# Graph layer with a mixture of experts on one core: the edge-row gathers run two groups ahead of the segment sums instead of four

## The reference

```
msg = feat[src]
agg = segment_sum(msg, dst, n)              # edges sorted by dst
deg = segment_sum(ones, dst, n)
x = x + feat @ W_self + (agg / max(deg, 1)) @ W_neigh + b        # feat = layernorm(x)
xn = layernorm(layernorm(x)) * gamma + beta
w = softmax of the two largest of (xn @ Wr + br)
x = x + sum over e of w[e] * (gelu(xn @ W1[e] + b1[e]) @ W2[e] + b2[e])
```

## Time and profile before

| | us |
|---|---|
| median of three runs | 1588.26 |
| lowest and highest | 1587.45, 1598.54 |
| span of the profiled execution | 1546.9 |
| mean granted TensorE clock | 0.908 |
| busy: TensorE, VectorE, ScalarE, GpSimd | 1199.9, 867.0, 426.8, 944.1 |

### The profile page before, as it was taken

How to read it: one execution, slowest core, us unless ns; L and a number is a source line. 1 busy time by engine, 2 the same in 40 slices (tenths; PEclk the granted TensorE clock), 3 DMA queues, 4 the chain that set the end, 5 groups by cost and what they waited for, 6 DMA issues and landing times.

```text
span 1546.9 us, 22459 instructions
## 1 busy us (share of the span) xinstructions
PE 1199.9 (78%) x6492; PEld 1041.8 (67%) x6493; DVE 867.0 (56%) x2814; ACT 426.8 (28%) x803; POOL 944.1 (61%) x1023
## 2 busy tenths in 40 slices
PE   0377988888977798989889888677858775879857
PEld 0266777867866676877778777566747764778747
DVE  6745556665564655656565565554636553545426
ACT  5412222222322332332332323213313210211111
POOL 6756656666566666566655657665665566666642
PEclk9788999999997899999999999788978897999979
DMA  9798777755454565555554555464565556656545
GB/s 335 232 297 247 244 230 239 238 166 173 152 166 124 164 190 160 181 172 171 188 182 157 181 157 164 135 191 133 165 204 157 167 158 199 201 165 222 167 139 175
DMA packets 175355, 289.69 MB, mean 187 GB/s; under 512 B 25600, under 2 KB 105344, under 8 KB 175104
## 3 DMA queue, kind: packets, MB, share of 16 engines
q1 hardware_dynamic: 124288, 156.38, 30.6%
q0 software_dynamic: 45504, 124.36, 27.3%
q10 hardware_dynamic: 5440, 7.47, 1.4%
HBM read 231.43 MB, written 56.68 MB: 186 GB/s over the span
## 4 chain that ended last, share of the span: by engine, by line
PE 33%; DVE 28%; another core or an unknown queue 21%; issue 12%; DVEq 2%; POOL 2%; DMA 1%; SPq 0%; ACT 0%; POOLq 0%; ACTq 0%
PE bank L1040 9%; PE bank L964 8%; PE bank L1066 6%; DVE agg L1311 5%; PE bank L1074 4%; DVE heap L1468 4%; DVE onehot L1257 3%; PE bank L952 2%; PE bank L993 1%; PE bank L995 1%; DMA heap<-in_x 1%; DVE nstats L1339 1%; DVE xf L1334 1%; DVE agg L1337 1%
## 5 line engine op out<-in xcount | busy, mean ns | idle before, releaser
L689 POOL DMA_INDIRECT ring<-feature_table,src_sb x760 | 742.3, 977 | 468.3 <-issue 194.6
L964 PE MATMUL bank<-ring,onehot 128*128 128x257 f32 x1552 | 404.0, 403 | 73.5 <-DMA rows<-in_x,src_sb 40.9
L964 PEld LDWEIGHTS bank<-ring,onehot 128*128 128x128 f32 x1552 | 312.1, 203 | 131.7 <-issue 83.4
L1468 DVE TENSOR_TENSOR heap<-bank,b_sb 128x512 f32<-128x512 f32 x145 | 100.1, 690 | 342.1 <-remote 249.7
L1066 PE MATMUL bank<-heap 128*128 x712 | 193.5, 418 | 60.4 <-issue 18.1
L1040 PE MATMUL bank<-row_t,heap 128*128 128x128 f32 x1424 | 195.9, 294 | 38.8 <-DVE heap L1468 19.3
L1040 PEld LDWEIGHTS bank<-row_t,heap 128*128 128x128 f32 x1424 | 186.6, 208 | 46.2 <-issue 45.0
L866 ACT ACTIVATE heap<-heap 128x512 f32<-128x512 f32 x145 | 91.6, 632 | 453.7 <-DVE heap L1468 312.7
L1066 PEld LDWEIGHTS bank<-heap 128*128 128x128 f32 x712 | 142.4, 208 | 86.0 <-issue 66.3
L1040 PE MATMUL bank<-dst_i,heap 128*128 128x128 f32 x896 | 115.8, 284 | 32.8 <-DVE heap L1468 25.9
L1257 DVE TENSOR_TENSOR onehot<-iota,target 128x512 f32<-128x512 f32 x196 | 134.3, 685 | 6.9 <-DVE xf L1328 3.5
(11 more groups left out here) (190 smaller groups left out, 1258.1 us busy)
## 6 DMA issues: line engine op xcount, KB each, us to landing
heap<-in_w SPq DMA_DIRECT2D x145, 512.0 KB
expert_out<-empty_row SPq DMA_DIRECT2D x68, 256.0 KB
ring<-feature_table,src_sb POOLq DMA_INDIRECT x760
row<-expert_rows SPq DMA_DIRECT2D x89, 128.5 KB
xf<-in_x SPq DMA_DIRECT2D x49, 128.0 KB
ff<-feature_table SPq DMA_DIRECT2D x49, 128.0 KB
expert_out<-inside SPq DMA_DIRECT2D x45, 128.0 KB
expert_out<-y_out SPq DMA_DIRECT2D x44, 128.0 KB
```

What stands on the lines that cost most here:

```text
L689: pool.indirect_dma_start(group_row(t, i)[:, 0:D], None, x if t < RAW else table, bass.IndirectOffsetOnAxis(src_sb[:, k:k + 1], 0)).then_i ...
L964: last = pe.matmul(bank[t % 2][:, 0:D + 1], onehot[:, q, i, :], group_row(t, i), start=(i == 0), stop=(i == GT - 1))
L1468: dve.tensor_tensor(hid[S.slot(u, 2)], hidden_b[:, :].rearrange("p (k t) -> p k t", k=HK), b1_sb[:, bass.ds(e, 1), :].rearrange("p o k -> ...
```

## The change

From group 10 on, the gather of group t waited until group t - 4 was summed, which is the group whose slot of the ring it takes. Now it waits until group t - 2 is summed. The ring keeps its four slots, and nothing else is changed; groups 6 to 9 wait as before.

```diff
 GT = 4
 GS = 4
+ROWS_AHEAD = 2
 LC = 7
...
             def gather(t):
                 g, q = NG - 1 - t, t % GS
                 if t >= RAW:
-                    pool.wait_ge(summed, (t - GS if t - GS >= RAW else t - RAW) + 1)
+                    pool.wait_ge(summed, (t - ROWS_AHEAD if t - GS >= RAW else t - RAW) + 1)
                 if t >= GS:
                     pool.wait_ge(gathered[q], 16 * GT * (t // GS))
```

## The result

The time falls from 1589.47 us to 1576.36 us (medians of four runs each); the ratio is 0.9891, 95% interval 0.9848 to 0.9933. The forecast was 1613 us, slower. The profiled execution after has a span of 1576.2 us and so stands at its own median. That of before, with 1546.9 us, stood 41 us under its median, so the two profiles can't be subtracted from one another. (The execution profiled after took 1578.0 us for its span of 1576.2, so only 1.8 us lie around a span.

The account below looks back on a forecast made before the run. TensorE and VectorE were taken to set each group's step, gathers running beside it. Stalls of 36.8 us less 12 given back made 24.8, added to the 1588.3 us median: 1613 us, range 1592 to 1648.

Parts of the forecast that it names:

- The edit really takes away room: Gathers from group 10 on: they start 11.6 us later on average over groups 17 to 195, losing about two thirds of their room.
- Start: Groups 10 to 12: gather 10 must wait for sum 8, 4.9 us later, all of it on the path.
- Bunches: Sums close together on TensorE: nine groups from 11 on lack the needed 7.0 us, together 13 us.
- the list: New gather starts carried through group by group: 28.6 us; 36.8 with later semaphore releases; 88.8 with two clocks mixed, too high.
- Given back: Behind late sums TensorE often waits anyhow, so a third of 36.8 us comes back: -12 us.
- two groups are enough: Rival, chance 0.30: nearly every stall is given back; +4 to +15 us, about 1597 us.
- Other work behind the gathers on GpSimd: Takes and row loads move later with the gathers: 3 us once for a take, not added; row loads 0.
- not slower: Rival, chance 0.05: in 85 to 150 us later gathers leave the DMA engines to weight loads; 1580 us.
- It does nothing: Rival, chance 0.02: GpSimd never was four groups ahead, so the edit changes nothing; 1588 us.
- delays compound: Rival, chance 0.13: stalls make GpSimd's later work later and TensorE's clock lower; 36.8 plus up to 50 us, 1640 to 1677.
- Late semaphores: Waits on TensorE's sums: releases come 2.1 us on average after the recorded end, taking 28.6 us to 36.8.
- The flight: From a gather's last issue to its landing: taken as 2 us, within a need of 7.0 us per group.

Follow-up runs that it names:

- r4_null: Kernel before with the run-ahead constant written out as 4, the same instructions; ratio 1.0019 to the kernel before.
- early2: Kernel before with run-ahead 2 for groups 10 to 29 only, 4 behind them; ratio 1.0046.
- mid2: Kernel before with run-ahead 2 for groups 30 to 149 only, 4 elsewhere; ratio 1.0054.
- late2: Kernel before with run-ahead 2 from group 150 on only, 4 ahead of it; ratio 0.9922.
- late3: Kernel before with run-ahead 4 up to group 149 and 3 from 150 on; ratio 0.9981.
- scat_early: Kernel before with run-ahead 2 everywhere and, from slot 150 on, scatter pairs two slots earlier in GpSimd's order; ratio 1.0099.
- pause8: Kernel before, run-ahead 4; GpSimd waits for the last issue's landing once eight gather, scatter and take issues would be passed; ratio 0.9957.
- threes: scat_late with gathers from group 150 on released in threes by one sum (distances 2, 3 and 4); ratio 1.0607 to the kernel before.
- r3: Kernel before with run-ahead 3 for all groups from 10 on; ratio 0.9975.
- takes_first: Kernel before, run-ahead 4, with the takes ahead of the scatter pair in slots from 150 on; ratio 0.9979.
- scat_late: Kernel before, run-ahead 4, with scatter pairs from slot 150 on two slots later in GpSimd's order; ratio 0.9878, repeated as 0.9944.
- start3: Kernel before with run-ahead 3 for groups 10 to 29 and 2 behind them; ratio 0.9852.
- three_two: Kernel before with run-ahead 3 up to group 149 and 2 behind; ratio 0.9950.

## Why the prediction was wrong

- **"The edit really takes away room", and the stalls.** Right in kind. Start: sum 10 ended some 9 us later (105.5 against 95.4 in before and 96.4 in r4_null), not 4.9. Bunches: group 61 waits 6.4 us where 4.3 was forecast. TensorE's idle time before sums rose by 55 us, above the list's 28.6 and 36.8 and under its upper bound of 88.8. So the direct cost wasn't over-sized.
- **"Given back: I take a third."** Too small. In the profiles with 2 at the start, sum 29 ends at 238 to 243 us, with 4 at 238 to 241: of the 9 us at most 2 are left. From sum 29 to sum 149 the mean is 893 us over four executions with 2 and 887 over nine with 4, without early2, mid2 and the kernels with pauses. By the timed ratios early2 and mid2 stand at +7 and +9 us (0.0046 and 0.0054 of 1590), each with one change back from 2 to 4 in it, which showed as 11 to 20 us at one place in their profiles, so the stages by themselves cost less. For this part of the kernel, sign and size were those of the rival "two groups are enough". One of the prediction's own signs of being wrong came true with it: the idle time before sums grew and the end did not.
- **The step that failed: "Other work behind the gathers on GpSimd."** I asked only whether takes and scatters that come later would be missed by their readers, put down 3 us for the takes and 0 for the row loads, and never asked whether they now come too early. The trace of before has these waits, though none of its rows was shown: 27.1 us in seven waits at L697 (r4_null: 35.8). The earlier trace rows gave only the scatters' durations, and the waits that I took from GpSimd's view were those of the gathers alone. Without these waits the work between sums 150 and 190 is 16 to 20 us shorter in the profiles: with 4 the stretch takes 320 to 338 us (mean of before, r4_null, early2 and mid2: 331), with 2 it takes 309 to 319 (mean of five: 315), with 4 and moved scatters 309 to 313 (mean of three: 311). late2 alone gives 0.9922. The kernel late3, with next to no such waits but little gain, says that the waits are not the whole of this term.
- **The rival "not slower"** had the right sign and nearly the right time (1580 against 1576), but not the place or the mechanism: it was to be decided in 85 to 150 us, by weight loads. early2, which has the change there, is slower. "It does nothing" falls with r4_null; "delays compound" is seen only with 1, and with scat_early in small.
- **Late semaphores.** I priced the "remote" releases as a delay that run-ahead 2 would meet more often. There are fewer of them after: 91.1 us before gathers against 117.5. At the waits and runs of the late stage they come together with TensorE's unexplained pauses, so they look like a sign of the cost that the change takes away (not shown by a run of its own), and I read them as a cost that it would add.
- **The end.** "0" was wrong: the stretch from the end of sum 195 to the end of the span is 74 to 81 us with 2 there and 69 to 73 with 4, some 6 us more. I didn't follow this further.
- **The flight.** I took 2 us from the end of the last issue to the landing, and wrote that the trace shows no landing. pause8's waits show it: 2.7 us of idle time on average, of which some 0.3 us pass in any case between two issues, so 2.4 us. The updates of the gathers' semaphores in the trace say the same: the last one comes 1.9 us (pause8) to 2.3 us (after) behind the end of the last issue, median, and 2.2 us in r4_null. The term was of the right size. The formula of the Trainium skill, DMA: Bandwidth & Descriptors, section Anatomy of one DMA, gave 2.3 us for 128 KB from its start. From the start of an issue, 0.95 us earlier, these rows give 2.8 to 3.4 us for an indirect gather of 128 rows, rather more.

**Shown**: the place (from group 150), and that it hangs on when GpSimd meets the scatters there: moving them alone brings the gain with run-ahead 4 and turns it into a loss with 2. **Supported, not settled**: that the waits for rows are paid for, and that the price arises in the runs of issues without a pause behind them. For the runs: threes, pause8, and a count of the runs of 12 or more issues that begin between 1100 and 1400 us, a window chosen afterwards. Each of the eight kernels at 0.985 to 0.995 without pauses (after among them) has two. r3 (0.9975) has three, late3 and takes_first (both 0.998) have five, before, r4_null, early2, mid2 and scat_early have four to six, and threes has nine. Against a clean verdict: over the whole kernel scat_late has hardly fewer issues from the ninth place on than late3 (100 and 106), the number of runs was not set by itself in any kernel without pauses, and threes changes two things. **Open**: why the other engines stop. The DMA engines aren't full in most of those windows (share 0.31 to 0.52, though 0.96 in one of r4_null), and the weight loads' median time to landing is the same with 4, 3 and 2. The Trainium skill, NOTIFIC — the notification-queue block, section The block in one page, names stalling the producer of the records as one of three things that the block can do when a queue of records overflows; no run here shows whether that happens. Also open is why three groups ahead at the start gain 8 us over four and over two.

## What to carry to other kernels

On an in-order queue, a run-ahead for one kind of work is a run-ahead for all the work between. Before you change it, list every wait on that queue, also those of the other instructions, and ask of each whether it is too early as well as whether it is too late. Where the bound is a stage, change the constant stage by stage before you explain it: one kernel with 2 from group 150 on said more than all comparisons of whole profiles. The best kernels here are start3 (0.985, run-ahead 3 up to group 29, then 2) and run-ahead 4 with late scatters (0.988 and 0.994). They ran on different chips; the interval of start3 (0.9811 to 0.9894) overlaps that of the first and not that of its repeat (0.9914 to 0.9974), and three_two, which begins and ends like start3, came to 0.995. So start3's lead isn't sure.

## What the runs showed of the hardware that was not expected

Beside long runs of GpSimd's indirect DMAs the other engines stand nearly still for some microseconds. Whether the runs cause it is what stayed open above. In r4_null, from 150 to 1480 us, TensorE is busy 0.92 of the time beside issues 3 and 4 of a run, 0.93 beside 5 and 6, 0.77 beside 7 and 8, 0.48 beside 9 and 10 and 0.14 beside 11 and 12; in threes 0.93, 0.90, 0.85, 0.55 and 0.11. It isn't the same everywhere: in scat_late 0.57 beside 9 and 10 and 0.43 beside 11 and 12. Behind a run of nine or more and a pause of up to 3 us it is back at 0.83 (r4_null) and 0.89 (threes) over the next four issues. In mid2, beside 20 issues from 1128 us on, a sum whose rows had long landed goes like this:

```profile
1144.47 0.85 PE L965 MATMUL bank<-ring,onehot 128*128 128x257 f32 x2
1146.98 0.38 PE L965 MATMUL bank<-ring,onehot 128*128 128x257 f32 x1 [1.66 <-issue]
1149.78 0.59 PE L965 MATMUL bank<-ring,onehot 128*128 128x257 f32 x1 [2.42 <-issue]
1151.90 0.59 PE L965 MATMUL bank<-ring,onehot 128*128 128x257 f32 x1 [1.53 <-issue]
1154.71 0.59 PE L965 MATMUL bank<-ring,onehot 128*128 128x257 f32 x1 [2.22 <-issue]
```

Matmuls of one sum, which otherwise follow each other in under 0.3 us, stand 2 to 3 us apart. The granted clock of the 10 us from 1145 is 0.67 and of the next 10 us 0.50, with the DMA share at 0.45 and 0.40:

```profile
1145.00:1155.00 10.00, 2.17 (x6) 0.90 (x4) 1.70 (x4) 0.00 (x0) 6.56 (x7) 0.67 0.45 131
1155.00:1165.00 10.00, 7.00 (x17) 5.24 (x17) 5.96 (x24) 1.83 (x5) 4.20 (x5) 0.50 0.40 131
```
